# A gate bias by matmul: 2 rows of the array, or 128 rows of which 126 are zero

## The reference

```python
Wh = W[:, :D]
Wz = W[:, D:]
leak = 1.0 - alpha
def step(h, z_t):
    gate = jax.nn.sigmoid(h @ Wh.T + z_t @ Wz.T + b)
    h_new = jnp.tanh(h * leak + gate * z_t)
    return (h_new, h_new)
_, hs = jax.lax.scan(step, h_t, jnp.swapaxes(z, 0, 1))
```

## Time and profile before

| | |
|---|---|
| time, median of 3 runs | 999.38 us (998.52 to 999.75) |
| span of the profiled execution | 1155.6 us |
| the profiled execution's own time | none is given beside the span |
| PE busy | 910.9 us, 79% |
| DVE busy | 716.7 us, 62% |
| ACT busy | 516.3 us, 45% |
| POOL busy | 275.5 us, 24% |
| bias matmuls | 64, of 9550 |
| mean granted TensorE clock | 0.879 |

### The profile page before, as it was taken

The page is one execution under the profiler, slowest core; times in us unless marked ns, Lnnn a source line. Parts: engine busy times, 40 slices in busy tenths (PEclk is TensorE's granted clock), DMA queues, the critical chain, the costliest instruction groups (busy, mean ns, idle before and its releaser), DMA issues.

```text
span 1155.6 us, 29134 instructions
## 1 busy us (share of the span) xinstructions
PE 910.9 (79%) x9550; PEld 633.8 (55%) x9550; DVE 716.7 (62%) x2491; ACT 516.3 (45%) x1431; POOL 275.5 (24%) x318
## 2 busy tenths in 40 slices
PE   2178769976999589986899779995999859998653
PEld 2067338843687247852588336862578426874432
DVE  5246447855777287754778457773878547657754
ACT  3155226632475145732466225742467324653333
POOL 1500730056002530045100550035300560005000
PEclk7599979987999789987999879996899879999955
DMA  7782323332243222532233322532223322322010
GB/s 239 246 256 78 124 73 93 112 108 75 72 130 124 88 66 72 142 100 78 81 102 103 115 69 65 145 114 83 73 66 111 107 77 75 106 88 74 10 29 19
DMA packets 91746, 115.24 MB, mean 100 GB/s; under 512 B 10930, under 2 KB 81108, under 8 KB 91604
## 3 DMA queue, kind: packets, MB, share of 16 engines
q1 hardware_dynamic: 77028, 73.43, 22.0%
q0 software_dynamic: 13856, 39.86, 10.7%
q10 hardware_dynamic: 720, 0.05, 0.1%
HBM read 56.68 MB, written 56.62 MB: 98 GB/s over the span
## 4 chain that ended last, share of the span: by engine, by line
PE 40%; DVE 16%; another core or an unknown queue 16%; ACT 10%; issue 10%; DMA 5%; POOL 2%; SPq 1%; DVEq 0%; ACTq 0%; POOLq 0%
PE bank L1127 36%; DVE pre L974 3%; PE bank L1250 3%; DVE hid_low L919 3%; DMA x_pair<-x_slots_even 3%; DMA x_pair<-x_slots_odd 2%; POOL x_slots_even L547 1%; DVE prod L906 1%; DVE zr L961 1%; ACT hid_high L674 1%; SPq L427 1%; ACT th L685 1%; DVE hs_low L981 1%; ACT hist L696 1%
## 5 line engine op out<-in xcount | busy, mean ns | idle before, releaser
L974 DVE TENSOR_TENSOR_SCAN pre<-th,zr 128x128 f32<-128x128 f32 x256 | 108.3, 423 | 232.2 <-ACT th L685 220.1
L1127 PE MATMUL bank<-hs_high,gwt_high 128*128 128x32 f16 x1024 | 81.2, 181 | 119.6 <-ACT hs_high L695 96.9
L685 ACT ACTIVATE th<-bank 128x64 f32<-128x64 f32 x256 | 59.5, 232 | 255.2 <-remote 164.6
L529 POOL TENSOR_TENSOR fence_pool<-zeros 128x1 f32<-128x1 f32 x48 | 12.3, 256 | 673.4 <-DVE is_low L869 353.5
L1127 PE MATMUL bank<-xe_high,w1e_high 128*128 128x128 f16 x768 | 161.3, 227 | 5.2 <-DVE xe_low L892 2.7
L1127 PEld LDWEIGHTS bank<-hs_high,gwt_high 128*128 128x128 f16 x1024 | 65.9, 100 | 171.7 <-ACT hs_high L695 125.7
L1127 PE MATMUL bank<-xe_low,w1e_high 128*128 128x128 f16 x768 | 159.3, 221 | 0.9 <-issue 0.9
L1127 PE MATMUL bank<-xe_high,w1e_low 128*128 128x128 f16 x768 | 158.9, 220 | 0.2
L695 ACT ACTIVATE hs_high<-pre 128x64 f16<-128x64 f32 x256 | 66.5, 260 | 188.0 <-DVE pre L974 176.8
L1127 PE MATMUL bank<-xs_high,w_high 128*128 128x512 f16 x256 | 109.6, 428 | 20.4 <-DVE prod L906 19.9
L1127 PE MATMUL bank<-xs_low,w_high 128*128 128x512 f16 x256 | 110.3, 431 | 2.8 <-issue 2.8
(11 more groups left out here) (162 smaller groups left out, 2307.4 us busy)
## 6 DMA issues: line engine op xcount, KB each, us to landing
x_pair<-x_slots_even SPq DMA_DIRECT2D x48, 256.0 KB
y_slots_even<-y_pair SPq DMA_DIRECT2D x48, 256.0 KB
x_pair<-x_slots_odd SPq DMA_DIRECT2D x48, 256.0 KB
y_slots_odd<-y_pair SPq DMA_DIRECT2D x48, 256.0 KB
x_tok<-in_x_dram SPq DMA_DIRECT2D x32, 256.0 KB, 5.3
out_dram<-o_tok SPq DMA_DIRECT2D x128, 64.0 KB, 1.7
x_slots_even<-zeros POOLq DMA_DIRECT2D x1, 3072.0 KB, 14.9
x_slots_odd<-zeros POOLq DMA_DIRECT2D x1, 3072.0 KB, 12.5
```

Source lines behind the costliest of these rows:

```text
L529: nc.gpsimd.tensor_tensor(fence_pool[:], zeros[:, 0:1], zeros[:, 1:2], ALU.mult).then_inc(s_fence, 1)
L685: nc.scalar.activation(flat3(th[:, s % 2, :, :, 1]), gate_sums(s), ACT.Tanh, scale=0.5 / UP).then_inc(s_th, 1)
L974: dve.tensor_tensor_scan(every(pre[:, s % 2]), every(th[:, s % 2]), every(zr[:, s % 2]), 0.0, ALU.mult, ALU.add).then_inc(s_pre, 1)
L1127: return pe.matmul(out_ap, w, mov, start=start, stop=stop, skip_group_check=True)
```

## The change

The stationary tile `gb` gets 128 rows, all zero but the first two, and the 2-row tile of ones is gone. The moving operand is a view of `ones16`: its first 32 columns, repeated 8 times with step 0, so 128 rows by 8 x 32 columns. The memset of `ones2` becomes one of `gb`, and the last instruction that builds the bias writes into `gb[0:2]`. No instruction is added, removed or moved on any engine, and all waits stay; one line fewer at the top shifts the line numbers by one.

```diff
--- before.py
+++ after.py
@@ -121,8 +121,7 @@
         gb_hi = sb("gb_hi", [2, C], F16)
         gb_lo = sb("gb_lo", [2, C], F16)
         gb_lo2 = sb("gb_lo2", [2, C], F16)
-        gb = sb("gb", [2, C], F16)
-        ones2 = sb("ones2", [2, HALF * NB], F16)
+        gb = sb("gb", [P, C], F16)
         al = sb("al", [P, KC])
         leak = sb("leak", [P, KC])
         ident = sb("ident", [P, P])
@@ -1069,7 +1068,7 @@
             def constants():
 
                 dve.wait_ge(s_small, 16 * 3)
-                link(dve.memset(ones2[:], 1.0))
+                link(dve.memset(gb[:], 0.0))
                 link(dve.memset(th[:], 0.0))
                 link(dve.tensor_scalar(leak[:], al[:], -1.0, 1.0, ALU.mult, ALU.add))
 
@@ -1077,7 +1076,7 @@
                 link(dve.tensor_copy(gb_hi[:], gb_full[:]))
                 link(dve.tensor_tensor(gb_lo[:], gb_full[:], gb_hi[:], ALU.subtract))
                 link(dve.tensor_scalar(gb_lo2[:], gb_lo[:], ident[0:2, 1:2], None, ALU.mult))
-                link(dve.scalar_tensor_tensor(gb[:], gb_hi[:], ident[0:2, 0:1], gb_lo2[:], ALU.mult, ALU.add))
+                link(dve.scalar_tensor_tensor(gb[0:2, :], gb_hi[:], ident[0:2, 0:1], gb_lo2[:], ALU.mult, ALU.add))
                 assert done[0] == N_CONST
 
             def recurrence_setup():
@@ -1211,6 +1210,7 @@
 
                 g = b.g - back
                 n = b.n - back
+                ones_all = ones16[:, 0:NB].rearrange("p (a b) -> p a b", a=1).broadcast_to([P, HALF, NB])
                 if n == 0 and half == 0 and hf == 0:
                     pe.wait_ge(s_gwlo, 2)
                     pe.wait_ge(s_const, N_CONST)
@@ -1220,7 +1220,7 @@
                 for jc in range(KC):
                     cols = slice(jc * P, (jc + 1) * P)
                     dst = gate_ps[hf][:].rearrange("p (t k b) -> p t k b", k=KC, b=NB)[:, :, jc, :]
-                    mm(dst, gb[:, cols], ones2[:].rearrange("p (t b) -> p t b", b=NB), jc == 0, False)
+                    mm(dst, gb[:, cols], ones_all, jc == 0, False)
                     pairs(dst, lambda a, k: gwt[a][:, KC + k, cols],
                           lambda c, k: zs[c][:, half, hf * HALF:(hf + 1) * HALF, k, :], False, False, range(KC))
```

## The result

The changed kernel took 990.74 us, the median of four runs (990.13 to 993.37), beside 999.57 us (998.52 to 999.87, four runs) for the kernel before, measured beside it. The ratio is 0.9922, with an interval from 0.9902 to 0.9943: 7.8 us faster by the ratio, 8.8 by the medians. The forecast was 989.4 us, in a range from 985.5 to 995.5.

The account below looks back on a forecast made before the run. TensorE and the recurrence chain take turns setting the time. Of 13.1 us of pauses, 3.3 + 3.2 + 0.6 + 0.8 + 2.0 = 9.9, say 10 us, reaches the end: 999.4 - 10.0 = 989.4 us, range 985.5 to 995.5.

Parts of the forecast that it names:

- "remote" waits: ScalarE's gate tanh waits 164.6 us in 32 places for something unnamed; timed executions were taken to hardly have them.
- The pause, 0.21 us for each bias matmul: Array stands around each 2-row bias matmul in the gate fills, half ahead, half behind; 64 x 0.205 = 13.1 us.
- rival C: Pauses stay, coming from something of the bias matmul other than its rows; 999.4 us, chance 0.06.
- What it adds, 0 of at most 7 us: Larger weight load, repeated view of ones and larger memset cost nothing; the view at most 7 us.
- Rival E: Slower: the bias matmul's repeated run of ones is read slowly, 1007 us at four times the pace; chance 0.05.
- u = 12: Fill at this unit number in all 8 sections: PE late by 1.2 us, 0.40 each counts, 3.2 us.
- u = 2: Fill at this unit number in all 8 sections: PE late by 3.6 us, whole 0.41 counts, 3.3 us.
- u = 8: Fill at this unit number: VectorE's routing leaves 0.1 each in sections 1 to 6, 0.6 us; sections 7 and 8, 0.8.
- Section end: Fill at a section's end, 8 times: ScalarE's 0.29 us idle bounds the gain, 0.25 each, 2.0 us.
- Rival B: All 13.1 us comes through, as VectorE and ScalarE have slack in timed executions; 986.3 us, chance 0.12.
- rival D: Pauses go, but the recurrence chain sets the pace more often than traced; half the gain, 994.5 us, chance 0.11.
- By less than 6: Sign on the whole kernel: a gain under 6 us would make the reading of the path wrong, not the pause's.

Follow-up runs that it names:

- the kernel with ones of its own: Changed kernel, but the bias matmul reads its own 128x256 tile of ones instead of the repeated view; 1149.65 us, ratio 0.9929 to the kernel before.
- the kernel with constant places: Changed kernel with expert weights at constant addresses instead of registers, bias matmul 128 rows in odd sections and 2 in even; 985.04 us, ratio 0.9856 to the kernel before.
- before once more: The kernel before, unchanged, run again as a control; 1154.41 us, ratio 0.9989.

## Why the prediction was right, step by step

- **What bounds, and the "remote" waits.** That they are absent in executions of 999 us was an assumption; the profile of after has none, so the sum could be taken off the median as it stood. It mattered less than I had thought: in the batch of 1156 us the kernel with ones of its own gained 0.7% as well.
- **The pause, 0.21 us for each bias matmul.** Right, at both clock levels, and it stands at each change between matmuls of at most 64 rows and taller ones. The reading by elimination from the earlier trace rows held: rival C (nothing goes) falls by the fills of the kernel after, and the 64- and 65-row kernels show the edge itself.
- **What it adds, 0 of at most 7 us.** Right: the full load of 100 ns hides, the repeated view costs nothing. Rival E falls by the kernel with ones of its own.
- **u = 12, 3.2 us.** Measured 3.3. Right, late by 1.2 us meant that all of 0.41 counts.
- **u = 2, 3.3 us.** Wrong in size: 1.4 us. "PE is late by 3.6 us; the whole 0.41 counts" was an argument on the state's readiness alone. TensorE has two sides, the array and the queue that feeds it. In sections 1 to 6 the queue is stopped until ScalarE has done `xs_high`, and its register operations behind that were hidden by the very pause that the change took away. They were not in the rows I had read, since they count as no engine's busy time. Most of the saving counts in sections 7 and 8 only, 0.33 us and 0.27, and 0.13 in each of the six others.
- **u = 8, 0.6 + 0.8 us.** Measured 0.6 in all. For sections 2 to 6 nothing came, where I took 0.1. VectorE, whom I had named, is in it, but not through the scan of the earlier trace rows: its `xe_low` ahead of the step lets TensorE's queue go on, and the register operations set the time from there; without them VectorE still takes all but 0.1, as the kernel with constant places shows. Sections 7 and 8 paid 0.4 and more. Section 1 was later by 0.3 to 0.5 in the two profiles with all fills at 65 or 128 rows (6.48 and 6.27 us, against 5.98 and 5.99 with 64 and 32 rows), with `xe_low` 0.3 later in that of after; but the kernel with two rows through the view has 6.27 as well, so the change need not be the cause.
- **Section end, 2.0 us.** Measured 2.4. Two errors that nearly cancel: I counted eight ends, but one of the eight fills stands ahead of the first step and only seven lie between two steps; and the bound of 0.29 us for each was too low, since 0.4 came in several (7.06 to 6.68 us, section 2). The rows show why. The kernel after, all engines, at the end of section 2:

```profile
371.74 0.60 PE L1250 MATMUL bank<-ident,x_pair 128*128 128x128 f32 x4
...
372.32 0.24 ACT L695 ACTIVATE hist<-pre 128x64 f32<-128x64 f32 x1
...
372.47 0.58 ACT L634 ACTIVATE xe_high<-bank 128x512 f16<-128x512 f32 x1
...
373.83 0.44 PE L1250 MATMUL bank<-ident,x_pair 128*128 128x128 f32 x2 [0.20 <-DVE xe_low L891]
```

And with 64 rows:

```profile
371.34 0.60 PE L1250 MATMUL bank<-ident,x_pair 128*128 128x128 f32 x4
...
371.51 0.24 ACT L695 ACTIVATE hist<-pre 128x64 f32<-128x64 f32 x1
...
372.06 0.60 ACT L634 ACTIVATE xe_high<-bank 128x512 f16<-128x512 f32 x1 [0.30 <-PE bank L1250]
...
373.43 0.55 PE L1250 MATMUL bank<-ident,x_pair 128*128 128x128 f32 x3 [0.20 <-DVE xe_low L891]
```

In both, `xe_high` starts 0.72 to 0.73 us after the transposes and TensorE goes on 2.09 us after them; the chain moved as a whole. ScalarE's idle time of 0.30 us went to nothing, but more was to be had: in the kernel after `xe_high` starts 0.15 us after `hist` started, that is 0.09 before `hist`'s recorded end. Idle time in the earlier trace rows is counted from recorded ends; the slack between starts was 0.55 - 0.15 = 0.40 us.

- **The sum.** Forecast 9.9, by places 7.6, by the ratio 7.8 (5.7 to 9.8). What was wrong is mostly u = 2 (1.9 us too much) and u = 8 (0.8 too much), against 0.4 too little at the section end. That the two times differ by 1.3 us only, and not by 2, is a little luck: the medians are 8.8 us apart. Rival B's 986.3 lies below all four runs and rival D's 994.5 above them.
- **The signs I had named.** z, bias, z at one pace: yes. The step behind u = 2 sooner by 0.4: no, 0.13 in sections 1 to 6. The one behind u = 8 sooner by 0.4 and the one behind that by 0.1 to 0.2: no, in sections 2 to 6 not sooner at all. "By less than 6" did not come about, though the interval just reaches it. So the two signs that concerned the path behind u = 2 and u = 8 failed, and the time was right in spite of them.

## What to carry over

Look for matmuls of 64 or fewer rows in a stream of tall ones: each cost 0.21 us here, at 2.4 GHz, in the distances of starts and not in any busy time, and filling up with zero rows to 65 or 128 took it away for nothing; where it can't be filled up, put the short ones together. Before a saving on TensorE is counted as whole, look behind it for the last wait that stopped its queue and for the register operations that follow it, which the pause may have been hiding, and not only at the data that the next step needs. Slack before an instruction is measured between starts in two places of the same chain; the idle time that a profile prints can be less than what there is.

## What the runs showed of the hardware

- The pause belongs to the change between a matmul of at most 64 rows and one of at least 65: 0.10 us in, 0.10 to 0.11 out at 2.4 GHz, the same for 2, 32 and 64 rows. At each change the weight load is not run beside the matmul ahead (0.20 us behind its start with 64 rows, together with it with 65). The Trainium skill, TensorE: Matmul & The Clock Gate, section Why this matters for your kernels, has a single 32-row matmul take as long as one of 128 rows; the recorded durations agree (0.27 to 0.28 us for either), and in this stream of tall ones it costs 0.21 us more.
- A moving operand that repeats 32 columns eight times is read at the plain pace (0.11 us for 256 columns).
- Weight addresses worked out in registers cost 0.057 us ahead of every third expert matmul where the queue has no lead (0.237 us of queue for three matmuls of 0.168), and with constants in their place the distances were plain.
- The kernel before took 999 us in some batches and 1156 in another, and the profiles differ in two stretches: from the step behind the u = 12 fill to the end of the section, 35.3 to 35.6 us in sections 1 to 6 and 56 to 59, with nearly all of the tanh's "remote" waits there (150 of 159.2 us in the profile of before once more); and ahead of the first step, 155 to 159 us and 176 to 177. The kernel before itself had both, so the variant is not the cause. What ScalarE waits for is open.
